# Splitting 125-partition transfers into 112 + 13 partitions, and up products over 64 rows instead of 128, in a fused graph network kernel

## The reference

```python
edge_index = jnp.stack([src, dst])
x = _layernorm(x + _L0_gnn_ref(x, edge_index, ...))                 # relu(x@W1+b1)@W2, then GCN aggregation
x = _layernorm(x + _L1_gnn_ref(x, edge_index, edge_weight, ...))    # two GCN convolutions, relu between
x = _layernorm(x + _L2_gnn_ref(x, src, dst, ...))                   # attention: segment max, exp, segment sum
x = _layernorm(x + _L3_gnn_ref(x, src, dst, edge_attr_32, ...))     # message MLP over edges, update MLP over nodes
```

## Time and profile before

| | |
|---|---|
| median of three executions | 3422.74 us |
| the profiled execution | 3427.62 us |
| its span from first to last instruction | 3425.8 us |
| mean granted clock of the tensor engine | 0.88 |
| stores of dense blocks, 250 KB each | 100 |
| loads `l_b<-t_x`, 125 KB each | 50 |
| units (ACT line 1077) | 390 |

### The profile page before, as it was taken

How to read it: one execution, slowest core, us unless ns; L and a number is a source line. 1 busy time by engine, 2 the same in 40 slices (tenths; PEclk the granted TensorE clock), 3 DMA queues, 4 the chain that set the end, 5 groups by cost and what they waited for, 6 DMA issues and landing times.

```text
span 3425.8 us, 46836 instructions
## 1 busy us (share of the span) xinstructions
PE 2624.9 (77%) x11672; PEld 1509.4 (44%) x11672; DVE 2135.1 (62%) x4381; ACT 1449.7 (42%) x2720; POOL 2398.7 (70%) x1858
## 2 busy tenths in 40 slices
PE   3888898999999877566657885887588856666665
PEld 2444444555555766455534443444254423333332
DVE  6776777777777655455548885555599954333332
ACT  2555555666665222122224443555344433323232
POOL 6766777878882888688868886888322248888887
PEclk9989899999999999777889998999799978777777
DMA  2444442222222333244434443333255532222221
GB/s 55 91 99 100 97 77 44 45 49 50 48 50 64 86 80 81 62 95 93 97 83 106 105 109 79 88 90 85 68 135 134 132 86 61 57 51 56 56 52 29
DMA packets 552946, 267.84 MB, mean 78 GB/s; under 512 B 480705, under 2 KB 526475, under 8 KB 552692
## 3 DMA queue, kind: packets, MB, share of 16 engines
q1 hardware_dynamic: 472817, 219.51, 25.8%
q0 software_dynamic: 80000, 46.91, 8.7%
HBM read 160.05 MB, written 105.00 MB: 77 GB/s over the span
## 4 chain that ended last, share of the span: by engine, by line
POOL 44%; PE 20%; issue 16%; DVE 9%; DMA 8%; SPq 2%; ACT 0%; DVEq 0%; POOLq 0%; ACTq 0%
POOL g_row L674 29%; POOL out_rows L681 7%; POOL l_a L674 7%; DMA t_x<-x_r 5%; PE bank L857 5%; PE pair L836 5%; PE pair L837 4%; PE bank L781 4%; DMA l_b<-t_x 2%; PE bank L848 1%; DVE x_r L1470 1%; SPq L549 1%; DVE rT L1485 1%; DVE ss L1399 1%; DVE ss_b L1427 1%
## 5 line engine op out<-in xcount | busy, mean ns | idle before, releaser
L674 POOL DMA_INDIRECT g_row<-t_x,gidx x600 | 803.6, 1339 | 243.4 <-issue 203.7
L1077 ACT ACTIVATE hid<-pair,b_up 128x1000 f32<-128x1000 f32 x390 | 425.6, 1091 | 204.8 <-PE pair L837 199.0
L858 PE MATMUL bank<-hid,w_dn 128*64 128x500 f32 x780 | 417.2, 617 | 0.0
L857 PE MATMUL bank<-hid,w_dn 128*64 128x500 f32 x780 | 417.1, 617 | 0.0
L674 POOL DMA_INDIRECT g_row<-in_x,src_i x200 | 263.3, 1317 | 122.2 <-issue 62.5
L674 POOL DMA_INDIRECT l_a<-in_x,dst_i x200 | 259.1, 1295 | 119.3 <-issue 60.6
L836 PE MATMUL pair<-xT,w_top 128*128 128x500 f32 x570 | 318.1, 642 | 2.2 <-ACT hid L1077 1.5
L674 POOL DMA_INDIRECT g_row<-t_h,gidx x200 | 258.5, 1293 | 80.3 <-issue 60.7
L837 PE MATMUL pair<-xT,w_bot 128*128 128x500 f32 x570 | 307.2, 622 | 0.0
L674 POOL DMA_INDIRECT info_r<-node_info,src_i x200 | 256.7, 1284 | 62.3 <-issue 60.6
L681 POOL DMA_INDIRECT out_rows<-n_r,fidx x200 | 250.7, 1253 | 64.7 <-issue 60.4
(11 more groups left out here) (260 smaller groups left out, 5707.1 us busy)
## 6 DMA issues: line engine op xcount, KB each, us to landing
x_in<-in_x_cols SPq DMA_DIRECT2D x105, 250.0 KB
out_rows<-x_r SPq DMA_DIRECT2D x100, 250.0 KB
t_x<-x_r SPq DMA_DIRECT2D x75, 250.0 KB
l_k<-keep_row SPq DMA_DIRECT2D x150, 125.0 KB
t_x<-n_r SPq DMA_DIRECT2D x150, 125.0 KB
l_a<-t_x SPq DMA_DIRECT2D x150, 125.0 KB
t_h<-h_r SPq DMA_DIRECT2D x50, 250.0 KB
l_k<-on_row SPq DMA_DIRECT2D x50, 250.0 KB
```

Of the source, the lines that this page charges most:

```text
L674: return g.indirect_dma_start(out=to, out_offset=None, in_=table, in_offset=bass.IndirectOffsetOnAxis(ap=index[:, tile:tile + 1], axis=0), ...
L857: T.matmul(run.down[0:D, 0:CH], w_dn[a.stage][:, 0:D], hid[a.b2][:, 0, :], start=True, stop=True)
L858: T.matmul(run.down[D:128, 0:CH], w_dn[a.stage][:, 0:D], hid[a.b2][:, 1, :], start=True, stop=True)\
L1077: A.activation(hid[a.b2][:, :, :], run.up[a.b2][:, :, 0:CH], ACT.Relu, bias=b_up[:, a.stage:a.stage + 1]).then_inc(Cn["hid"], 1)
```

## The change

Three edits:

1. The up products contract 64 partitions instead of 128: the lower one takes rows 0 to 63 of `w_top` and of the columns, the upper one rows 64 to 127 of `w_bot` and of the columns. The rows left out are the zeros of the weight tiles, so the result is the same.
2. A dense store is two transfers, of 112 and of 13 partitions. All that count them (32 for 16) follow.
3. Level G's load of `l_b` is two transfers, of 112 and of 13 partitions; its semaphore counts 80 per chunk.

```diff
+WIDE = 7 * 16
...
-        G_ld, G_st = in_turn("ld", 4, 64), in_turn("st", 4, 16)
+        G_ld, G_st = in_turn("ld", 4, 80), in_turn("st", 4, 16)
...
                 sp.wait_ge(Cn["rows"], i * 3 + 3)
-                sp.dma_start(dense_out[i - (NI + 4)], x4_r[par][:, :]).then_inc(out_sem[par], 16)
+                for rows in (slice(0, WIDE), slice(WIDE, R)):
+                    sp.dma_start(dense_out[i - (NI + 4)][rows], x4_r[par][rows, :]).then_inc(out_sem[par], 16)
...
-                                (l_k[q][0:D + 1, :], bc(decay_d, k, D + 1)), (v4(l_b[q][:, :]), rows_of(t3_d)[k])],
+                                (l_k[q][0:D + 1, :], bc(decay_d, k, D + 1)),
+                                (v4(l_b[q][0:WIDE, :]), rows_of(t3_d)[k][0:WIDE]),
+                                (v4(l_b[q][WIDE:R, :]), rows_of(t3_d)[k][WIDE:R])],
...
-                at_least(pool, G_ld[q], h * 64 + 64)
+                at_least(pool, G_ld[q], h * 80 + 80)
...
-                pool.wait_ge(out_sem[r], 16 * len(range(r, NB, 2)))
+                pool.wait_ge(out_sem[r], 32 * len(range(r, NB, 2)))
...
-                        T.matmul(run.up[a.b2][:, 0, 0:CH], w_top[a.stage][:, :], columns[:, :], start=True, stop=True)
-                        T.matmul(run.up[a.b2][:, 1, 0:CH], w_bot[a.stage][:, :], columns[:, :], start=True, stop=True)\
+                        T.matmul(run.up[a.b2][:, 0, 0:CH], w_top[a.stage][0:D, :], columns[0:D, :], start=True, stop=True)
+                        T.matmul(run.up[a.b2][:, 1, 0:CH], w_bot[a.stage][D:128, :], columns[D:128, :], start=True, stop=True)\
                          .then_inc(Cn["up"], 1)
...
-                                v = 16 * stored(NI + 4, a.i) if known else at_m * 16 - 16 * ((NI + 5) // 2 - a.par)
+                                v = 32 * stored(NI + 4, a.i) if known else at_m * 32 - 32 * ((NI + 5) // 2 - a.par)
...
-                    at_least(dve, G_ld[q], h * 64 + 64)
+                    at_least(dve, G_ld[q], h * 80 + 80)
```

## The result

| | before | after |
|---|---|---|
| median | 3421.66 us (4 executions) | 3384.71 us (4 executions, 3376.38 to 3386.22) |
| the profiled execution, its span | 3427.62, 3425.8 us | 3376.38, 3374.6 us |
| mean granted clock | 0.880 | 0.863 |

The ratio is 0.9891, 95% interval 0.9861 to 0.9921: faster by 37 us. The forecast was 3344 with a range of 3326 to 3376, so the direction was right and the size was not. Some 40 of the forecast's 79 us are missing. The two profiled executions lie further apart than the medians: before's is at the upper end of its kernel's times (3410.67 to 3427.66), the changed kernel's is the shortest. So the traces show 51.2 us of gain where the medians show 37, and the 14 us between the two can't be placed by any trace.

A forecast was written before the change was run, and what follows sets the result against it. PE was taken to bound the dense blocks, GpSimd levels A, C and M, VectorE nearly level G. -58.7 - 6 - 14 = -78.7 gave 3348.9 from the profiled 3427.62, 3344 on the median's scale; range 3326 to 3376.

The forecast's parts named there:

- Up products: Dense units: the two 64-row products overlap, a pair costing 0.99 us instead of 1.68, saving 0.69 per unit.
- rival of switches without overlap: Up products run in turn and each unit pays two shape changes of 0.15 us; 3459 us, chance 0.04.
- Seam, -58.7: Before level A: the dense part shortens until GpSimd, which stood 58.66 us there, becomes the bound; -58.7 us.
- First blocks, -6: Up to 111 us: eight up pairs on the chain each lose one product, passed on to later work; -6 us.
- Elsewhere, 0: 111 to 480 us bound by stores landing; C and D bound by GpSimd, ends allowed 5 us; 0.
- Level G, -14: Level G: split transfers drain faster, leaving VectorE at 5.72 us per chunk, 286 us in all; -14 us.
- own range of 3332 to 3356: Whole kernel: range of the forecast case, chance 0.62, from spreads in G, ends of C and D, and first blocks.
- 0.2% of noise: Whole kernel: a measurement was said to tell 0.2%, 7 us, from no change.
- splitting costs its issues: Level G rival: splitting gains nothing, 3358 us, or 3378 if all added issues show; chance 0.12.

The follow-up runs named there:

- e8: Kernel before with 64-row up products, both over rows 0 to 63 so neither runs on disjoint rows; 3511.54 us, one execution.
- e1: Kernel before with only the 64-row up products, no transfer split; 3366.13 us, ratio 0.9822.
- e2: Kernel before with only the two transfer splits (dense store and `l_b`), up products over 128 rows; 3449.03 us, ratio 1.0072.
- e5: Changed kernel with one added wait: GpSimd's level G multiply starts only after VectorE's `rT` of the slot before; 3352.05 us, ratio 0.979.
- e6: e1 (no splits) with the same added wait of the multiply for `rT` as e5; 3364.42 us, ratio 0.9827.
- e4: Changed kernel with GpSimd's multiply over 8 columns instead of 500, no candidate since messages stay unscaled; 3343.41 us, ratio 0.9754.
- e11: e5 with the five stores of each isolated block also split into 112 and 13 partitions; 3321.98 us, ratio 0.9721.

## Why the prediction was wrong

- **Up products: right.** A pair at 0.99 us forecast, 1.04 measured. e8, one execution, shows that it is the side-by-side that pays, and also that the rival of switches without overlap was a real one: by its price (84 us more in the profile) it was underrated at 36.
- **Seam, -58.7: right.** 58.66 us to 0, because GpSimd takes over.
- **First blocks, -6: right in size, but not passed on.** The gathers of source rows end 8.2 us earlier (5.8 in e1). The gathers of level A begin only 1.8 us earlier, at 1007.4 for 1009.2.
- **Elsewhere, 0: two errors that cancel.** I took GpSimd's rate as given. The 200 gathers of `info_r` went from 317.4 to 322.5 us, in every kernel with 64-row products (321 to 323) and not in e2 (316.3). Its cause is open. So level A ends 58.7 us earlier, not 64.7, and the levels B to D, from which nothing was expected, gave 7.9 us. Up to the end of level D the forecast was -64.7 and the trace has -66.6: the agreement is partly luck. e1, which has only this part, was forecast by it at 3358 and took 3366.
- **Level G, -14: the step that failed.** It read: if the transfers drain faster, VectorE is left with 5.47 us for a chunk, 5.72 with handshakes. The first half held in the main: the late third chunk is gone, SP's load of a dense block takes 0.7 to 1.9 us there for 2.0 to 3.2 in all but the first two of before, and VectorE's scans, after the first, wait 4.3 us for the multiply in place of 11.6. The second half took VectorE's busy time as a constant. It isn't one: a busy time holds the waiting for GpSimd's multiply (295.86 us between the first and the last scan of the changed kernel, 262.71 before, with 623 and 622 instructions), and how much depends on *when* that multiply starts. Landing earlier moved it from 6.7 to 4.9 us after `w_r`'s end (medians; before they lie anywhere from 3 to 10), right onto the next one, and gave 39 of 50 `w_r` some 0.95 us more each. These are 37.0 us. Shorter waits of the scans give back 7.3 of them, other VectorE operations 3.0; 2.8 more were not traced, and 23.9 are left as the loss.
- **The size of that term was too large as well.** With the multiply behind `rT` level G is 11.6 us shorter than before (e5), and the whole is at 3352, inside the forecast's own range of 3332 to 3356. But the splits have only 7.5 of these (e6 to e5), half of 14; the other 4.1 come with the up products and the wait. More was not there for a split to take: in before the scans waited 11.6 us for the multiply. That 11.6 is near 14 is luck.
- **The sum of the trace.** The traces differ by -51.2 us where -78.7 were forecast, so 27.5 are missing. Level G is off by 37.9 (23.9 lost for 14 won). The other way, 10.4 came that no term had: 1.9 up to the end of level D, 4.3 from there to level G's first scan and 4.2 after its last. The further 14 us, between the profiled executions and the medians, stay open.
- **Ranges.** The own range of 3332 to 3356 is narrower than the bounds it names: they add up to 3325 to 3364. The 0.2% of noise was too narrow as well: the interval of the result is 0.3% to either side.
- **The clue was in the rows of before.** The multiply that stood 6.70 us for `l_b` I read as lateness only. Some collisions are there already: the norm of every third unit (`x_r<-y_r`) takes 0.86 us on average in level G of before and 0.98 in e1, where it is 0.69 in e5. I never asked where a multiply that came sooner would fall. No rival had it: "splitting costs its issues" ended at 3378 and had no more VectorE time in it.
- **Clock.** It stood at 0.85 in level G for 0.92, after PE had become less busy there (239 of 309 us for 248 of 300), and at 0.97 in the dense part for 0.99. Level G did not pay for it: between its first and last scan VectorE is busy for 295.86 of 312.4 us, and the waits of VectorE there name PE for 1.6 us before and not at all after. The clock came back with the time: 0.94 in e5's level G, 0.92 in e4's. Elsewhere it was not tested by itself; PE has 3% of the chain.

The Trainium skill has the mechanism: "SBUF — State Buffer", section "Who interferes with whom", says that VectorE instructions with two SBUF inputs contend with a GpSimd instruction that reads SBUF, that the port pair they share is an exclusive lock, and that the order of issue decides which of the two is blocked. The trace agrees: `w_r` (both inputs in SBUF) ends 0.27 us after the multiply, while the reduction and `v_r` (one input in PSUM) that run in the multiply in e5 keep 0.67 and 0.42 us. The runs show the waiting, in both directions; that it is for a port is what the page adds. On the split, "DMA: Bandwidth & Descriptors", "Rules for kernel authors", advises against cutting a transfer into partition halves; for 125 partitions cut into 112 + 13 the measurement decides the other way, by SP's 15 us per block that became under 8 (e11) and 30 us of the whole.

## What to carry to other kernels

When a change makes something land earlier, ask what then starts earlier, and beside which instruction of the other engines it will run; VectorE and GpSimd with operands in SBUF are the pair to look at, and an operation whose duration is 3 times its usual one names the collision. Placing the second engine's work with one wait, into a stretch where the first reads PSUM or one operand, can be worth more than the transfer change itself. Do not read a busy time as the least an engine needs: it can hold waiting for another. And before crediting a transfer's size, look at how long its issuing engine holds it: 250 KB over 125 partitions in pieces of 256 bytes held SP mostly for 2.8 to 4.1 us, 112 + 13 partitions for 0.9 to 2.3 (e11). A dense store, 250 KB over 125 partitions in rows of 2048 bytes, held it for 0.3 us whole and 0.87 split: the same cut costs issue time there.

## What the runs showed of the hardware

- A `w_r` of 0.39 us that meets a multiply of 1.24 us takes 1.33 to 1.41 us in the rows shown; the two in lockstep made a nearly stable period of 6.5 us where 5.57 was free.
- Two products over disjoint row halves start within 0.01 us of each other and take 1.04 us as a pair; over the same half 1.87 (e8, one execution), more than the 1.68 over 128 rows.
- From the fifth step on, level G's scans are 5.5 to 5.7 us apart in e4, except for two steps of 8.7 and 8.8 us, the 24th and the 36th. All kernels have them, at 8.1 to 10.0 us; the distance of twelve chunks fits a turn of the loop in the instruction lists. That a turn costs some 3 us is argued, not shown: no run was made on it.
